# Slot terms, their transposition and the one-hots of a graph-attention edge loop, made for two blocks of edges at once

## What is computed

```python
h = (x @ W).reshape(n, H, C)                       # H = 4 heads, C = 128
a_src = (h * att_src[None]).sum(-1)
a_dst = (h * att_dst[None]).sum(-1)
a_edge = (e * att_edge[None]).sum(-1)
alpha = a_src[src] + a_dst[dst] + a_edge
alpha = jax.nn.leaky_relu(alpha, NEG_SLOPE)
amax = jax.ops.segment_max(alpha, dst, num_segments=n)
ex = jnp.exp(alpha - amax[dst])
denom = jax.ops.segment_sum(ex, dst, num_segments=n)
msg = h[src] * (ex / (denom[dst] + 1e-16))[:, :, None]
out = jax.ops.segment_sum(msg, dst, num_segments=n)
```

## Time and profile before

| | |
|---|---|
| median of 3 runs | 3154.42 us (3150.92 to 3158.08) |
| the profiled execution, its own time | 3153.78 us |
| its span | 3152.0 us |
| edge loop of the second graph layer | from 982 to 1436 us of the span |
| mean granted TensorE clock over the span | 0.879 of full speed |
| busy over the span: PE, DVE, ACT, POOL | 79%, 52%, 27%, 19% |

### The profile page before, as it was taken

How to read it: one execution, slowest core, us unless ns; L and a number is a source line. 1 busy time by engine, 2 the same in 40 slices (tenths; PEclk the granted TensorE clock), 3 DMA queues, 4 the chain that set the end, 5 groups by cost and what they waited for, 6 DMA issues and landing times. The chain is left out here.

```text
span 3152.0 us, 30953 instructions
## 1 busy us (share of the span) xinstructions
PE 2501.1 (79%) x10585; PEld 1589.8 (50%) x10585; DVE 1649.1 (52%) x3721; ACT 862.6 (27%) x1943; POOL 600.7 (19%) x566
## 2 busy tenths in 40 slices
PE   4877953999955888884577999999998669759867
PEld 1344443999943666662443455445544234534443
DVE  9999253121332888887235897709952522430000
ACT  2155110111111666662111465116621100100110
POOL 0000057344302444431110000000001001012221
PEclk9999965999977888887598999999999889779888
DMA  4000353567724455450534453215424040459995
GB/s 125 0 1 17 119 155 99 181 213 255 254 75 118 131 145 139 135 110 24 180 112 148 177 190 112 79 54 183 160 82 141 0 151 11 179 194 350 345 331 180
DMA packets 198686, 445.51 MB, mean 141 GB/s; under 512 B 26537, under 2 KB 48025, under 8 KB 198052
## 3 DMA queue, kind: packets, MB, share of 16 engines
q1 hardware_dynamic: 156900, 344.65, 32.6%
q0 software_dynamic: 41632, 98.89, 12.1%
HBM read 396.75 MB, written 49.05 MB: 141 GB/s over the span
## 5 line engine op out<-in xcount | busy, mean ns | idle before, releaser
L2159 PE MATMUL psum<-x_res,HH 125*128 125x512 f32 (+1 forms) x960 | 351.7, 525 | 19.7 <-DVE x_res L2349 19.7
L2159 PEld LDWEIGHTS psum<-x_res,HH 125*128 125x128 f32 x960 | 181.6, 193 | 179.4 <-issue 157.1
L1144 POOL DMA_INDIRECT recd<-edge_records,edge_slots x160 | 193.8, 1211 | 329.6 <-issue 323.2
L1504 POOL DMA_INDIRECT hg<-HT,srcidx x196 | 190.5, 972 | 305.1 <-PE psum L1624 176.2
L1665 ACT ACTIVATE hg<-hg,ex 128x129 f32<-128x129 f32 x784 | 235.1, 389 | 1.6
L1624 PE MATMUL psum<-hg,Dh 128*125 128x258 f32 x784 | 231.3, 459 | 4.8 <-DVE ACC L1567 3.0
L2149 PE MATMUL psum<-W,XO 128*125 128x512 f32 x480 | 212.1, 603 | 0.0
L1624 PEld LDWEIGHTS psum<-hg,Dh 128*125 128x125 f32 x784 | 176.9, 232 | 45.7 <-issue 6.7
L1178 PE MATMUL psum<-xgT,w 128*128 128x192 f32 x1024 | 175.6, 331 | 1.7 <-DMA w<-in_L_ffn_w 1.7
L1178 PEld LDWEIGHTS psum<-xgT,w 128*128 128x128 f32 x1024 | 169.1, 193 | 5.9 <-DMA w<-in_L_ffn_w 3.4
L1187 PE MATMUL psum<-sums_room,w 128*128 128x192 f32 x1024 | 170.3, 326 | 0.0
(11 more groups left out here) (507 smaller groups left out, 3989.9 us busy)
## 6 DMA issues: line engine op xcount, KB each, us to landing
wd<-in_L_ffn_W_down SPq DMA_DIRECT2D x30, 2560.0 KB
w<-in_L_ffn_w SPq DMA_DIRECT2D x64, 1024.0 KB, 11.7
MK<-CT SPq DMA_DIRECT2D x80, 625.0 KB
wu<-in_L_ffn_W_up SPq DMA_DIRECT2D x8, 2730.0 KB, 17.4
rows<-ROWS POOLq DMA_DIRECT2D x24, 625.0 KB, 7.3
w<-in_L_ffn_W SPq DMA_DIRECT2D x18, 512.0 KB
t<-in_L_ffn_tv_W SPq DMA_DIRECT2D x16, 512.0 KB
targets<-DROW SPq DMA_DIRECT2D x49, 128.0 KB
```

The source lines that it names most:

```text
L1144: pool.indirect_dma_start(out=g.recd, out_offset=bass.IndirectOffsetOnAxis(ap=g.posi[:, c:c + 1], axis=0), in_=g.E8[:, c, :], in_offset=No ...
L1504: pool.indirect_dma_start(out=hg[j % RING][:, c, :], out_offset=None, in_=g.HT, in_offset=bass.IndirectOffsetOnAxis(ap=g.srcidx[:, j * CH ...
L2159: return pe.matmul(flat[:, at:at + x1 - x0], HH[:, k, h * DH + c * 128:h * DH + c * 128 + 128], z[n % 4][:, x0:x1], start=(k == 0 and i < ...
```

## The change

Slot terms, transposition, copy to qT and one-hots are made once for a pair of blocks (p covers blocks 2p and 2p + 1; 25 pairs, the last with one block). The hg ring becomes one tensor with six places, so that one instruction can read two of them. q, q_parts, DT, mb and Dh are twice as wide; q and Dh have two buffers in place of three. qT has 96 rows in place of 48, and the selector `sel` (N4 = 2 CH NH = 32) grows with it; spread, look-up and sum of block j take their half of the pair's tensors. The searches, new maxima, look-ups, alphas, weights, sums and gathers stay one for each block.

The orders become:

- VectorE, even j: largest, new maximum, slot terms of the next pair, add sums, alpha. Odd j: largest, new maximum, add sums, alpha, one-hots of the next pair. Ahead of the loop: slot terms and one-hots of pair 0.
- TensorE transposes, and ScalarE copies, in even blocks alone.
- SP loads the targets of a pair with one DMA, three pairs ahead.
- POOL: the gathers of blocks 2 and 3 wait for the slot terms of pair 0, those of blocks 4 and 5 for those of pair 1. From block 6 on nothing changes.

```diff
     def pool_program():
         for j in range(NB):
             if j >= RING:
                 pool.wait_ge(*summed.at(j - RING + 1))
+            elif j >= 2:
+                pool.wait_ge(*rows.at(j // 2))
...
+    def dve_slot_terms(p):
+        n, first = chunks(p), 2 * p % RING
+        for j in range(2 * p, 2 * p + n // CH):
+            dve.wait_ge(*gathered[j % RING].at(64 * (j // RING + 1)))
+        found = hg[:, first:first + n // CH, :, HW:HW + NH].rearrange("p r c h -> p (r c) h")
+        step(dve.tensor_tensor(q[p % 2][:, 0:n, :], found, rec(p)[:, :, 2:6], ALU.add))
+        if p:
+            dve.wait_ge(*turned.at(p))
+        split(dve, step, q[p % 2][:, 0:n, :].rearrange("p c h -> p (c h)"),
+              [q_parts[:, k, 0:n * NH] for k in range(3)], q_rest[:, 0:n * NH]).then_inc(*rows.up())
...
+    def dve_onehots(p):
+        n = chunks(p)
+        cols = slice(0, n * 128)
+        dve.wait_ge(*loaded[p % 3].at(16 * (p // 3 + 1)))
+        if p >= 2:
+            dve.wait_ge(*looked.at(2 * (p - 1)))
+        dve.tensor_scalar(DT[p % 2][:, cols], drow[p % 3][0:TP, cols], g.pcol[0:TP, :], None,
+                          ALU.is_equal).then_inc(*onehot.up())
+        if p:
+            dve.wait_ge(*top.at(NH * 2 * p))
+        dve.tensor_scalar(mb[:, cols], drow[p % 3][0:TP, cols], g.pcol[0:TP, :], NEG, ALU.not_equal,
+                          ALU.mult).then_inc(*onehot.up())
+        if p >= 2:
+            dve.wait_ge(*summed.at(2 * (p - 1)))
+        dve.tensor_tensor(Dh[p % 2][:, 0:n, :], g.iota_tp[:, None, :].to_broadcast([128, n, TP]),
+                          rec(p)[:, :, 1:2].to_broadcast([128, n, TP]), ALU.is_equal).then_inc(*onehot.up())
...
-            if j + 2 < NB:
-                dve_slot_terms(j + 2)
+            if j % 2 == 0 and j // 2 + 1 < NP:
+                dve_slot_terms(j // 2 + 1)
             if j >= 2:
                 dve_add_sums(j - 2, tiles[j - 2])
             dve_alpha(j)
-            if j + 1 < NB:
-                dve_onehots(j + 1)
+            if j % 2 == 1 and j // 2 + 1 < NP:
+                dve_onehots(j // 2 + 1)
...
             if j + 1 < NB:
                 pe_spread(j + 1)
-            if j + 2 < NB:
-                pe_turn(j + 2)
+            if j % 2 == 0 and j // 2 + 1 < NP:
+                pe_turn(j // 2 + 1)
...
             act_rescale(j)
-            if j + 2 < NB:
-                act_rows(j + 2)
+            if j % 2 == 0 and j // 2 + 1 < NP:
+                act_rows(j // 2 + 1)
             act_weights(j)
```

More of the change, by code:

```diff
@@ L1482, in bank, with chunks, rec, half @@
         return g.PS[0:TP, k, :]
-    def rec(j):
-        return g.rec[:, j * CH:(j + 1) * CH, :]
+    def chunks(p):
+        return min(2, NB - 2 * p) * CH
+    def rec(p):
+        return g.rec[:, 2 * p * CH:2 * p * CH + chunks(p), :]
+    def half(j):
+        return j // 2 % 2, j % 2 * CH
     def tile_of(eng, j):
@@ L1493, in sp_program @@
     def sp_program():
[L1494 to L1497, removed]
+        for p in range(NP):
+            if p >= 3:
+                sp.wait_ge(*onehot.at(3 * (p - 2)))
+            n = chunks(p) * 128
+            sp.dma_start(drow[p % 3][:, 0:n], bcast(g.DROW[2 * p * BLK:2 * p * BLK + n], 128)
+                         ).then_inc(*loaded[p % 3].up(16))
     def pool_program():
@@ L1507, in pool_program @@
                                         ).then_inc(*gathered[j % RING].up(16))
[L1509 to L1516, removed]
@@ L1552, in dve_alpha @@
             dve.wait_ge(*expd.at(j - 1))
+        b, c0 = half(j)
         look = g.PS[:, 5, 0:CH * 8].rearrange("p (c k h) -> p c k h", c=CH, k=2)
-        step(dve.tensor_tensor(al[u][:], q[j % 3][:], look[:, :, 0, :], ALU.add))
+        step(dve.tensor_tensor(al[u][:], q[b][:, c0:c0 + CH, :], look[:, :, 0, :], ALU.add))
         step(dve.scalar_tensor_tensor(al[u][:], al[u][:], 0.2, al[u][:], ALU.mult, ALU.max))
@@ L1589, in dve_program, with pe_turn @@
         dve.wait_ge(*added.now())
[L1591 to L1594, removed]
+    def pe_turn(p):
+        pe.wait_ge(*rows.at(p + 1))
+        if p:
+            pe.wait_ge(*rowsT.at(p))
         pe.matmul(g.PS[0:3 * N4, 4, 0:128], q_parts[:].rearrange("p k n -> p (k n)"), g.identb[:],
@@ L1598, in pe_spread @@
     def pe_spread(j):
-        pe.wait_ge(*rowsT.at(j + 1))
+        b, c0 = half(j)
+        pe.wait_ge(*rowsT.at(j // 2 + 1))
         if j:
@@ L1608, in pe_look_up @@
     def pe_look_up(j):
-        b = tile_of(pe, j)
+        tile, (b, c0) = tile_of(pe, j), half(j)
         pe.wait_ge(*newmax.at(j + 1))
@@ L1613, in pe_look_up @@
         for c in range(CH):
-            ins = pe.matmul(g.PS[:, 5, c * 8:c * 8 + 8], DT[j % 2][:, c * 128:(c + 1) * 128], am(b),
+            ins = pe.matmul(g.PS[:, 5, c * 8:c * 8 + 8], DT[b][:, (c0 + c) * 128:(c0 + c + 1) * 128], am(tile),
                             start=True, stop=True)
@@ L1632, in pe_program @@
         pe_spread(0)
-        pe_turn(1)
         for j in range(NB):
@@ L1642, in pe_program, with act_rows @@
         pe_sum(NB - 1)
-    def act_rows(j):
-        act.wait_ge(*turned.at(j + 1))
-        if j >= 2:
-            act.wait_ge(*spread.at(j - 1))
-        act.activation(qT[j % 2][:], g.PS[0:3 * N4, 4, 0:128], ACT.Copy).then_inc(*rowsT.up())
+    def act_rows(p):
+        act.wait_ge(*turned.at(p + 1))
+        if p >= 2:
+            act.wait_ge(*spread.at(2 * (p - 1)))
+        act.activation(qT[p % 2][:], g.PS[0:3 * N4, 4, 0:128], ACT.Copy).then_inc(*rowsT.up())
     def act_rescale(j):
```

40 lines of the change are left out of this document (13 added, 27 removed).

## The result

The changed kernel took 3159.06 us (median of 20 runs, 3154.52 to 3165.91), the kernel before, measured beside it, 3152.86 (20 runs). The ratio is 1.0025 with a 95% interval of 1.0016 to 1.0034: slower by a quarter of a per cent, where 3150 us, a little faster, had been forecast. The profiled execution of the changed kernel took 3157.68 us (span 3155.9); that of before 3153.78 (3152.0).

A forecast was written before the change was run, and what follows sets the result against it. The prediction took a ring of gathers, late handoff, search, look-up, spread and sum to bound the loop. Middle -3, start 0 and end -1.5 us summed to -4.5, giving a median of 3150 us, full range 3128 to 3164.

The forecast's parts named there:

- What bounds the loop before: Edge loop: a ring of gathers, late TensorE handoff, search, look-up, spread and sum sets 8.70 us a block, not VectorE's work.
- the first rival: Edge loop: VectorE sets the pace after all, so 26 us go and the time is 3128 us; chance 17%.
- Slot terms and one-hots for two blocks: VectorE in the loop: fewer, wider instructions save 1.52 us a pair, 0.76 a block.
- What reaches the end: Middle of the loop: waiting blocks hide most of VectorE's saving; -3 us, bounds 0 and -16.
- New waits: Slot terms of a pair, needing its second block's gather: no wait, with 0.7 us or more to spare.
- the 0.2 of 8.6: Sign of a right reading: the loop's block period stays within 0.2 us of 8.6.
- The rival of the later gather wait: Early-handoff blocks: half of seven wait 2.1 us each for gathers, 7 us together, giving 3160 us; chance 10%.
- Where cover goes: VectorE after even blocks, now without one-hots before the next search: costs nothing, the wait for the handoff covers it.
- Transposition and copy: TensorE and ScalarE, once a pair: zero gain, -5 us as other end; ScalarE's wait ahead of its copy should halve.
- Start: First blocks of the loop, with paired slot terms and spaced gathers: 0 us, range -5 to +8.
- End: Last blocks, without gathers, where VectorE sets the pace: -1.5 us, bounds 0 and -2.

The follow-up runs named there:

- Group 5: Last group of runs: changed kernel with only VectorE's adding of sums ahead of slot terms, 1.0063; with transposition and copy also late, 0.9992; kernel before 3114.53 us.
- the ring of eight: Changed kernel with eight gather buffers in place of six: 3148.37 us, 1.0016 of the kernel before.
- the second trace of the changed kernel: Profiled execution of the changed kernel, unaltered, measured again beside later variants: 1.0038 of the kernel before.
- the fastest order: Changed kernel with even blocks' adding of sums ahead of slot terms, alpha behind them, transposition behind the sum, copy behind the weights: 0.9956, later 0.9992 of before.

## Why the prediction was wrong

**What bounds the loop before.** Right for the profiled run. Without gathers it runs 0.9% faster, at VectorE's list; in the group with prompt handoffs it took 3114.53 us, 1.2% less than the 3152.86 beside the changed kernel. The idea of the first rival, that VectorE sets the pace where the handoff is not late, holds there; its price does not, for pairing gained nothing even with no gathers (0.9926 for 0.9909). The page of the Trainium skill that was weighed in it (SBUF — State Buffer, "Who interferes with whom") says that DMA never contends with a compute engine. Group 5, with 0.7 us of delay in all, agrees with what the rival took from it; all other groups, with 1 us behind a row of issues and 12.6 us at the start of the ring of eight, do not.

**Slot terms and one-hots for two blocks.** Right: 1.33 us from first to last instruction in the block above (1.36 forecast), one-hots 2.26 (2.30), VectorE's busy time down 31.7 us (30 or more).

**What reaches the end.** -3 us, bounds 0 and -16. The ring of eight shows what pairing is worth when nothing new waits: 16.37 us for two blocks against 17.14 or 16.93, some 11 to 15 us over 38 blocks. So the bounds held, and the forecast lay near the wrong one.

**New waits: the step that failed.** "No wait, with 0.7 us or more to spare" compared two times after the end of the sum. The landing was put at 8.9 = 0.28 + 4.73 + 3.9. It came at 9.43 = 0.27 + 5.76 + 3.40: landing was over-priced by 0.5, the issue under-priced by 1.0, since the third issue takes 1.91 us while the doubled one-hots run (1257.51 to 1259.77). The slot terms were put at 9.65, with a handoff at 6.2. They were due at 7.62 (1263.43 after 1255.81), since the search began at 4.09. That term, 2 us out, decided. The late handoff was taken for all blocks; in even blocks of the new order the spread ends 1.5 us after the group begins, in every one of the middle, and its handoff comes 2.8 to 3.6 us after the group's start. In the block above the search follows the one-hots with no wait (1259.77, 1259.90). The rows were there. Three or four blocks were priced with that wait, and 21 of 22 had it. The 9.0 us that it made the middle lose were in part hidden in the total by the 5.5 that the start gained. The block period of 8.79 lies within the 0.2 of 8.6 that was named as a sign of being right, so that sign could not tell.

What is queued behind it had been named, the adding of sums and alpha. What was not followed is that the adding frees the banks of the next sum, and so that the wait closes a ring with the gather that the sum releases. The rival of the later gather wait gave 3160, and 3159.06 was measured. It named the right wait, but that its number came out is luck: it priced 7 us of waits, and there were 36 in 21 blocks (29.3 and 6.5), of which 9.0 remain in the middle after what pairing gave.

**Where cover goes.** "Nothing" was wrong as a rule: with no gathers VectorE waits 2.1 us a pair for TensorE, now that the even blocks have no one-hots. With gathers that was hidden by the ring.

**Transposition and copy.** Right that the scalings' wait is no loss: moving the copy alone gave nothing. ScalarE's wait did not halve (131 us in 43 waits before, the two lines together, 91 in 22 after).

**Start.** Forecast 0, range -5 to +8, and -5.5 us measured (-2.9 in the second trace of the changed kernel); first alpha at 1011.4 (forecast 1013, before 1016.46). Of the 5.4 us by which the fifth search came earlier, pairing without the spacing gave 3.8, and the spacing alone 2.6 and nothing in the ratio.

**End.** -1.5 forecast, +0.7 measured. The last blocks wait for TensorE, as without gathers.

## What to carry to other kernels

When a change makes a step wait for a later transfer, list what is queued behind it on its engine and follow each to the buffer that it frees: if one of them frees what releases that transfer, the wait is a term of a ring and comes back in every period. Take both times of such a race for each kind of block by itself, with the step's neighbours as they will be after the change; a mean over two kinds hid 2 us here. Put a step that may wait for a transfer behind those that free buffers: orders of this kind made the paired kernel 0.5 to 0.8% faster than unordered, and 0 to 0.4% faster than before, while the same order unpaired cost 1%, and the adding moved alone left it 0.6% slower than before where the handoff was prompt.

## What the runs showed of the hardware

TensorE's result reached other engines late while POOL issued indirect gathers, in the first measurement and in four of the five groups of runs: about 1 us after the last issue of a row of four, or 2.8 to 4.3 us after its start where the matmuls ended early in it, and in a row of 16 issues a look-up's result waited 12.6 us. In the fifth group it was never late, and what makes the difference is open. So a kernel tuned around it in one group of runs can lose its gain in another: the fastest order gave 0.9956 and 0.9992.

An indirect gather's issue took 1.91 us for 0.95 where it stood beside the one-hots of 1000 elements; with one-hots of 500 again, a group of four took 5.0 us for 5.7.

TensorE's granted clock in one period of the changed kernel, by stretches (length, busy PE, PEld, DVE, ACT, POOL, clock):

```profile
1257.50:1261.00 3.50, 3.50 (x18) 2.78 (x16) 3.36 (x7) 3.34 (x12) 2.89 (x3) 1.00 0.61 164
1261.20:1263.50 2.30, 0.00 (x0) 0.00 (x0) 1.87 (x9) 1.51 (x7) 1.69 (x3) 1.00 0.80 196
1263.60:1268.00 4.40, 3.50 (x26) 3.32 (x26) 2.50 (x12) 0.27 (x2) 2.66 (x3) 0.54 0.81 242
1268.00:1270.00 2.00, 2.00 (x5) 1.61 (x6) 1.39 (x5) 1.90 (x7) 0.00 (x0) 0.50 0.35 118
```

```profile
1263.57 1.52 PE L1632 MATMUL psum<-AM,DT 125*128 x8 [2.45 <-issue]
```

After 2.45 us without a matmul, ahead of the look-up at 1263.57, the clock stands at 0.5, the level of 1.2 GHz, until some way into the sum. That sum takes 5.16 us, the one before it, at 2.4 GHz, 3.70. In the middle of the changed kernel the odd blocks' sums, those in the ring, take 5.45 in the mean and the even blocks' 3.71. It is not the wait for the gather that does it, since the ring of eight has 5.30 and 3.71 too. Those 1.7 us are a part of the ring of 17.6. The middle of the changed kernel ran at 0.80 of full speed, that of before at 0.85.
